# Row-sum reciprocals of two 16-head attentions: four iterative reciprocals, or a guess by exponential and two corrections

## The chip, the cores and the metric

The kernel runs on 1 core of a Trainium2 chip. The metric is the device time of one execution in microseconds. TensorE is called PE in the views, VectorE DVE, ScalarE ACT, GpSimd POOL and SyncE SP.

## What is computed

Four layers in sequence on `x` of 4 sequences x 1024 tokens x 128 features. Each ends with `x = layernorm(x + layer(x))`. Layer 0 is a causal attention of 16 heads of 64, layer 1 an attention of 8 heads whose weights are gated (top 3 of 5 experts), layer 2 an attention of 16 heads with a bias by relative position, layer 3 a mixture of 16 experts. The change is in layers 0 and 2 alone, and there in the denominators of the softmax:

```python
def _L0_attn_ref(x, W_Q, W_K, W_V, W_O):
    ...
    masked = jnp.where(causal, scores, jnp.float32(-MASK_VAL))
    attn = jax.nn.softmax(masked / np.float32(np.sqrt(D_HEAD)), axis=-1)
    z = jnp.einsum('bacC,baCh->bach', attn, v)
    out = jnp.einsum('aeh,bach->bce', W_O, z)
    return out
def _L1_attn_ref(hidden_states, Wq, Wk, Wv, Wo, rel_bias):
    ...
    scores = jnp.einsum('bqhd,bkhd->bhqk', q, k) * SM_SCALE + bias
    attn = jax.nn.softmax(scores, axis=-1)
    out = jnp.einsum('bhqk,bkhd->bqhd', attn, v).reshape(b, s, H * DK)
    return out @ Wo
```

All arithmetic is in fp32. Products that need its precision are made of two halves (`ah` and `al`, `bh` and `bl`) in fp32r.

## The kernel before, in words

`pair_stage` runs layers 0 and 2, called s0 (causal) and s2 (biased) here; `gated_stage`, s1, runs between them, and the experts come last. A stage treats 32 pairs of heads: 4 sequences x 8 pairs. A pair has units `(c, j)`: query half `c` of 512 columns, key block `j` of 128. There are 16 units a pair in s2 and 12 in s0 (blocks over the diagonal are left out, and later ones are narrower). All units of one `c` are a pass, so each stage has 64 passes, numbered `s = 2g + c`.

Each engine runs its part of the same list of units in order, and semaphores tie them together. In a unit

- TensorE makes the scores of two heads in PSUM (`sT`, two buffers, L359 and L364), one or two blocks of products for the row maxima of the next pair (`mx`, one buffer, L340), and the product of the probabilities of two units before with the values (`pv`, L384). Jobs that share the single bank `misc` lie between: projections of the next pairs ("item", "v"), the column sums ("rs"), transposes and the output projection ("y"). A job waits until the last one's `misc` has been read (`misc_free`);
- VectorE reads the maxima (`maxima`: L548 and L551 in s0; L561 and L567 in s2), subtracts halves (L527) and, in s2, adds the near biases in PSUM before the exponential (`near_biases`, L610, units 0 to 4 and 11 to 15). Next come, where a pair's maxima are complete, their rows (L577 to L595);
- ScalarE takes the exponential of the scores (`exponentials`, L476) into one of four buffers `prob`, and copies PSUM to SBUF (`copy`, L426);
- POOL adds up the exponentials of a pass elementwise (L729), SBUF to SBUF, and in s0 masks the diagonal block (L714).

The denominator of a pass: when POOL has added the last unit, TensorE multiplies `psum_p` with ones into `misc` ("rs", L286), so that each of 128 partitions holds the sums of its head; ScalarE copies them into `recip` (L426); VectorE takes the reciprocal in four pieces of 128 columns, one a unit, at the start of the unit (`reciprocals`, L615), and later multiplies the copied `pv` in `z` with it (`normalize`, L621). `Pairs.jobs` writes the order: for the second pass of the pair before, "rs" is in unit 2, the reciprocals in units 3 to 6 and the product in unit 7; for a pair's own first pass they are in units `at1+2`, `at1+3` to `at1+6` and the next or last unit, where `at1` is 4 in s0 and 8 in s2 (so 10, 11 to 14 and 15 in s2). `y`, the output projection, waits for `z_done` once a sequence.

The order of the work is in these lists alone; nothing is planned at run time.

## Time and profile before

| | |
|---|---|
| runs | 4654.91, 4660.39 (median), 4664.32 us |
| profiled execution, its own time | 4659.69 us |
| its span in the profile | 4658.0 us |
| mean granted clock of TensorE | 0.946 |
| TensorE busy | 4061.7 us (87%) |
| VectorE busy | 3451.8 us (74%) |
| POOL busy | 2799.3 us (60%) |
| ScalarE busy | 1968.4 us (42%) |

By the exponentials at L476, s0's units run from 94 to 1281 us and s2's from 2807 to 4477 us. "Pair 12" below is the thirteenth of its stage; its first unit starts at 3436.7 us in s2.

How to read the views: the stretches give the time in which an engine had an instruction running. The view of the waits tells whose result ended an engine's idle time. The groups sum all instructions of one line, operation and tile: busy time, mean length of one, and idle time just before them. The view in time merges neighbours of one engine that are alike (x2, x3). What is recorded as the start of a VectorE or POOL instruction can lie before it moves data, so an instruction that waits for memory reads as a long one.

### The profile page before, as it was taken

The page shows a single profiled execution, that of the slowest core. Times are in us where ns is not written, and L with a number is a line of the kernel's source. Part 1 is how long each engine was busy: PE and PEld are TensorE (multiplying, and loading weights), DVE is VectorE, ACT ScalarE, POOL GpSimd, SP SyncE. Part 2 cuts the span into 40 slices and gives each one's busy share as a digit, 9 for nine tenths or more (in the row PEclk, how much of TensorE's full clock was granted, in tenths as well). Part 3 has the DMA queues.
Part 4 walks back from the last instruction along what each step waited for, and adds up shares of the span by engine and source line. Part 5 has one row for each costly group of instructions (what it writes and reads, how often), then busy time and mean ns, then how long its engine had stood idle before and what let it go on. Part 6 is the DMA issues. An engine that isn't in the chain of part 4 may idle for free. (4 is left out here: it accounts for less than half of the span.)

```text
span 4658.0 us, 63371 instructions
## 1 busy us (share of the span) xinstructions
PE 4061.7 (87%) x22554; PEld 2155.1 (46%) x22554; DVE 3451.8 (74%) x5816; ACT 1968.4 (42%) x3446; POOL 2799.3 (60%) x2036
## 2 busy tenths in 40 slices
PE   5999999999968889989899748999999999999964
PEld 3554544444444555555555324444444444444423
DVE  3777887868757777777877537887888788878836
ACT  2443443434434555455454313443444344434422
POOL 0655655646624777777887905665666566656640
PEclk6999999999978999999999959999999999999987
DMA  3000000000010000000000021211122121212111
GB/s 51 14 14 14 23 14 23 14 9 6 1 63 26 26 26 26 27 26 26 31 26 9 5 59 27 39 28 28 37 35 34 28 37 28 34 23 44 18 46 37
DMA packets 98041, 125.90 MB, mean 27 GB/s; under 512 B 28896, under 2 KB 76448, under 8 KB 97728
## 3 DMA queue, kind: packets, MB, share of 16 engines
q1 hardware_dynamic: 97728, 121.86, 12.2%
q8 instruction: 180, 2.95, 0.3%
q14 instruction: 133, 1.09, 0.1%
HBM read 103.69 MB, written 18.12 MB: 26 GB/s over the span
## 5 line engine op out<-in xcount | busy, mean ns | idle before, releaser
L729 POOL TENSOR_TENSOR s_psum_p<-s_psum_p,s_prob 128x1024 f32<-128x1024 f32 (+3 forms) x640 | 1350.0, 2109 | 418.9 <-ACT s_prob L476 379.9
L476 ACT ACTIVATE s_prob<-s_sT 128x1024 f32<-128x1024 f32 (+2 forms) x896 | 835.9, 933 | 969.5 <-DVE s_sT L610 477.3
L384 PE MATMUL s_pv<-s_prob,s_vp 128*64 128x512 f32 (+3 forms) x3584 | 890.4, 575 | 3.9 <-POOL s_prob L714 2.9
L729 POOL TENSOR_TENSOR s_psum_p<-s_prob 128x1024 f32<-128x1024 f32 (+1 forms) x128 | 286.9, 2241 | 574.7 <-ACT s_prob L476 572.1
L615 DVE RECIPROCAL s_recip<-s_recip 128x128 f32<-128x128 f32 x512 | 481.3, 942 | 100.3 <-ACT s_recip L426 100.3
L340 PE MATMUL s_mx<-s_bh,s_ah 64*128 64x512 f32 (+3 forms) x1792 | 390.1, 431 | 184.1 <-DVE s_bm L551 85.3
L1613 POOL TENSOR_TENSOR s_psum_p<-s_psum_p,s_prob 128x1024 f32<-128x1024 f32 x192 | 461.5, 2403 | 107.5 <-ACT s_prob L1336 105.5
L561 DVE CUSTOM_DVE_ANT_0 s_mx<-s_mx,s_strip 128x512 f32<-128x512 f32 x640 | 429.4, 712 | 111.8 <-PE s_mx L340 110.7
L1336 ACT ACTIVATE s_prob<-s_sT 128x1024 f32<-128x1024 f32 x256 | 262.4, 1025 | 583.8 <-PE s_sT L1200 583.7
L359 PE MATMUL s_sT<-s_ah,s_bh 64*128 64x512 f32 (+3 forms) x1792 | 414.5, 459 | 19.1 <-ACT s_prob L476 18.8
L551 DVE TENSOR_REDUCE s_bm<-s_mx 128x8 f32<-128x1024 f32 (+3 forms) x384 | 362.5, 944 | 50.5 <-PE s_mx L340 41.7
L1449 DVE SCALAR_TENSOR_TENSOR s_part<-s_sT,s_gate,s_part 128x128 f32<-128x128 f32 x945 | 287.6, 322 | 131.0 <-ACT s_part L1328 81.2
L340 PEld LDWEIGHTS s_mx<-s_bh,s_ah 64*128 64x128 f32 x1792 | 172.9, 189 | 415.3 <-DVE s_bm L551 165.6
L1493 DVE TENSOR_REDUCE s_bm<-s_mx 128x2 f32<-128x1024 f32 x214 | 261.5, 1222 | 136.6 <-PE s_mx L1165 135.7
L359 PEld LDWEIGHTS s_sT<-s_ah,s_bh 64*128 64x128 f32 x1792 | 168.8, 185 | 398.0 <-issue 217.2
L359 PE MATMUL s_sT<-s_al,s_bh 64*128 64x512 f32 (+3 forms) x1792 | 339.5, 374 | 0.0
L359 PE MATMUL s_sT<-s_ah,s_bl 64*128 64x512 f32 (+3 forms) x1792 | 339.0, 374 | 0.0
L364 PE MATMUL s_sT<-s_mr,s_rowsel 64*128 64x512 f32 (+3 forms) x1792 | 338.8, 373 | 0.0
L567 DVE TENSOR_REDUCE s_bm<-s_mx 128x2 f32<-128x1024 f32 x192 | 232.7, 1212 | 102.3 <-PE s_mx L340 101.9
L384 PEld LDWEIGHTS s_pv<-s_prob,s_vp 128*64 128x64 f32 x3584 | 178.1, 135 | 254.7 <-issue 223.9
L610 DVE TENSOR_TENSOR s_sT<-s_sT,s_near 128x512 f32<-128x512 f32 (+2 forms) x320 | 236.5, 739 | 65.0 <-PE s_sT L364 64.7
L1212 PE MATMUL s_pv<-s_prob,s_qkv 128*64 128x512 f32 x1024 | 280.8, 628 | 2.6 <-ACT s_z L1257 2.6
(251 smaller groups left out, 7535.9 us busy)
## 6 DMA issues: line engine op xcount, KB each, us to landing
s_strip<-bias_rows SPq DMA_DIRECT2D x256, 144.0 KB, 5.8
s_wr<-gated_weights SPq DMA_DIRECT2D x32, 960.0 KB, 4.8
s_near<-bias_rows SPq DMA_DIRECT2D x256, 48.0 KB, 2.0
x<-s_x SPq DMA_DIRECT2D x12, 512.0 KB, 3.2
s_x<-x SPq DMA_DIRECT2D x8, 512.0 KB, 4.8
gated_weights<-s_side_hi SPq DMA_DIRECT2D x8, 480.0 KB, 2.5
gated_weights<-s_side_lo SPq DMA_DIRECT2D x8, 480.0 KB, 2.9
s_x<-in_L_attn_x_dram SPq DMA_DIRECT2D x4, 512.0 KB, 4.6
```

The costliest lines, as they stand in the source:

```text
L340: last = mm(mx[:, hd, 0:hi], ah[heads(hd), g % 3, i * P:(i + 1) * P], bh[heads(hd), g % 3, c * CH:c * CH + hi], start=True, stop=True)
L359: mm(sT[:, k % 2, hd, lo:CH], key[heads(hd), r, keys], query[heads(hd), r, cols], start=n == 0, stop=False)
L364: last = mm(sT[:, k % 2, hd, lo:CH], rowsel[heads(hd), j if st.biased else 0, :], mr[heads(hd), g % 2, cols], start=False, stop=True)
L384: last = mm(pv[heads(hd), lo:CH], vp[:, g % 2, j, heads(hd)], prob[:, k % PR, hd, lo:CH], start=j == 0, stop=end)
L476: nc.scalar.activation(prob[:, k % PR, :, lo:CH], sT[:, k % 2, :, lo:CH], ACT.Exp, scale=st.scale).then_inc(exp_done, 1)
L551: nc.vector.tensor_reduce(bm[:, g % 2, :, i, 4 * c:4 * c + nblk], mx[:, :, 0:nblk * P].rearrange("p a (j n) -> p a j n", n=P), X, ALU.max)\
L561: last = nc.vector.tensor_tensor_reduce(out=mx[:, hd, :], in0=mx[:, hd, :], in1=strip[:, g % 2, hd, first:first + CH], scale=1.0, scalar=N ...
L615: nc.vector.reciprocal(cols, cols).then_inc(recip_done, 1)
L729: nc.gpsimd.tensor_tensor(out[:, :, lo:CH], src, p[:, :, lo:CH], ALU.add)\
L1212: last = mm(pv[heads(hd), :], qkv[:, g % 3, j, 2, heads(hd)], prob[:, k % PR, hd, :], start=j == 0, stop=j == NB - 1)
L1449: nc.vector.scalar_tensor_tensor(o, src, scale(s, e), o if e else more[:, to], ALU.mult, ALU.add).then_inc(p_dve, 1)
L1613: nc.gpsimd.tensor_tensor(out, src, p, ALU.add).then_inc(sum_done, 1)
```

## The change

`recip` still gets the sums by a copy. Right behind it ScalarE takes a guess of their reciprocals from the same bank: it reads the bits of the fp32 sums as an integer and takes `exp(127 ln 2 - 0.03 - ln 2 · bits / 2^23)`, which is 2 to the negative of a piecewise linear logarithm. With `t` the sum and `r` the guess, VectorE makes `t·r` (n0), ScalarE `(t·r - 1.5)²` (`squares`), VectorE `r·(square + 0.75)` (n1), `-t·r` (n2), `z·r` (n3) and `z·(2 - t·r)` (n4). All are whole passes of 128x512. `guess` and `square` have one buffer each. The bank `misc` is free for TensorE's next job after the guess (`guess_done`) and no more after the copy (`rs_read`). In the unit VectorE's reciprocal work now comes behind the near biases, the maxima and their rows. n0 is in the unit of the first reciprocal before, the square in the unit behind it, n1 and n2 in the second unit behind, n3 and n4 in the third. Two memsets set the bias columns `shifts`.

```diff
--- before.py
+++ after.py
@@ jobs
         for s, u in ((2 * g - 1, 3), (2 * g, rs1 + 1)):
             if s >= 0:
-                for n in range(4):
-                    out[u + n].append(("recip", s, n))
-                out[u + 4 if u + 4 < self.U else u + 3].append(("norm", s))
+                for n, later in enumerate((0, 2, 2, 3, 3)):
+                    out[u + later].append(("recip", s, n))
+                out[u + 1].append(("sq", s))
@@ tensor, misc_free
                 elif kind == "rs":
-                    pe.wait_ge(rs_read, of + 1)
+                    pe.wait_ge(guess_done, of + 1)
@@ scalar, misc_job
                     copy(recip[:, s % 2, :], misc[:, :]).then_inc(rs_read, 1)
+                    if s == 0:
+                        act.wait_ge(shift_set, 2)
+                    else:
+                        act.wait_ge(recip_done, 3 * s)
+                    nc.scalar.activation(guess[:, :], misc[:, :].bitcast(I32), ACT.Exp,
+                                         scale=-math.log(2.0) / 2 ** 23, bias=shifts[:, 0:1])\
+                        .then_inc(guess_done, 1)
@@ scalar
+            def squares(s):
+                act.wait_ge(near_one, s + 1)
+                nc.scalar.activation(square[:, :], square[:, :], ACT.Square, bias=shifts[:, 1:2])\
+                    .then_inc(sq_done, 1)
+
@@ scalar, units
                     if t[0] in MISC:
                         misc_job(t)
+                    elif t[0] == "sq":
+                        squares(t[1])
@@ vector
             def reciprocals(s, n):
-                dve.wait_ge(rs_read, s + 1)
-                cols = recip[:, s % 2, n * P:(n + 1) * P]
-                nc.vector.reciprocal(cols, cols).then_inc(recip_done, 1)
-
-            def normalize(s):
-                dve.wait_ge(recip_done, 4 * (s + 1))
-                dve.wait_ge(pv_read, s + 1)
-                out = z[:, (s // 2) % NZ, half(s % 2)]
-                tt(out, out, recip[:, s % 2, :], ALU.mult).then_inc(z_done, 1)
+
+                total, r, out = recip[:, s % 2, :], guess[:, :], z[:, (s // 2) % NZ, half(s % 2)]
+                fused = nc.vector.scalar_tensor_tensor
+                if n == 0:
+                    dve.wait_ge(rs_read, s + 1)
+                    dve.wait_ge(guess_done, s + 1)
+                    tt(square[:, :], total, r, ALU.mult).then_inc(near_one, 1)
+                elif n == 1:
+                    dve.wait_ge(sq_done, s + 1)
+                    fused(r, square[:, :], 0.75, r, ALU.add, ALU.mult).then_inc(recip_done, 1)
+                elif n == 2:
+                    dve.wait_ge(recip_done, 3 * s + 1)
+                    fused(total, total, -1.0, r, ALU.mult, ALU.mult).then_inc(recip_done, 1)
+                elif n == 3:
+                    dve.wait_ge(pv_read, s + 1)
+                    tt(out, out, r, ALU.mult).then_inc(recip_done, 1)
+                else:
+                    dve.wait_ge(recip_done, 3 * s + 3)
+                    fused(out, total, 2.0, out, ALU.add, ALU.mult).then_inc(z_done, 1)
@@ vector, units
             for g, u, k, c, j, todo in units():
-                for t in todo:
-                    if t[0] == "recip":
-                        reciprocals(t[1], t[2])
                 if st.near(c, j):
                     near_biases(k)
                 for t in late:
                     misc_job(t)
@@
-                    elif t[0] == "norm":
-                        normalize(t[1])
+                    elif t[0] == "recip":
+                        reciprocals(t[1], t[2])
```

At the end of a stage the last pass runs the same steps with nothing between them.

How the order of VectorE moves, at two places of a pair of s2. Names are the program's tiles; the ISA rows are reads of `mx`. First from the end of unit 4's read of `mx` to the first of unit 6's, before:

```order
L561 ISA s_bm 128x1
L615 RECIPROCAL s_recip<-s_recip 128x128
L567 TENSOR_REDUCE s_bm<-s_mx 128x2
L615 RECIPROCAL s_recip<-s_recip 128x128
L527 TENSOR_TENSOR s_bl<-s_misc,s_bh 128x512
L561 ISA s_mx,s_bm<-s_mx,s_strip 128x512
```

And now, where L583 and L589 read the maxima, L549 subtracts, and L641, L644, L647 are n0, n1, n2:

```order
L583 ISA s_bm 128x1
L589 TENSOR_REDUCE s_bm<-s_mx 128x2
L644 SCALAR_TENSOR_TENSOR s_guess<-s_square,s_guess 128x512
L647 SCALAR_TENSOR_TENSOR s_recip<-s_recip,s_guess 128x512
L549 TENSOR_TENSOR s_bl<-s_misc,s_bh 128x512
L583 ISA s_mx,s_bm<-s_mx,s_strip 128x512
```

The two reciprocals of units 5 and 6 are gone, and n1 and n2 stand together behind unit 5's read, ahead of unit 6's subtraction. Second the end of unit 12 to unit 15, before:

```order
L577 COPY s_m<-dcol 128x2x16
L581 TENSOR_TENSOR s_bm<-s_bm,delta 128x2x3
L586 TENSOR_REDUCE s_m<-s_bm 128x2x8
L615 RECIPROCAL s_recip<-s_recip 128x128
L610 TENSOR_TENSOR s_sT<-s_sT,s_near 128x2x384
L615 RECIPROCAL s_recip<-s_recip 128x128
L610 TENSOR_TENSOR s_sT<-s_sT,s_near 128x2x384
L595 TENSOR_TENSOR s_mr<-s_mx,constants 128x512 x2
L610 TENSOR_TENSOR s_sT<-s_sT,s_near 128x2x256
L621 TENSOR_TENSOR s_z<-s_z,s_recip 128x512
L610 TENSOR_TENSOR s_sT<-s_sT,s_near 128x2x256
```

And now, with the near biases at L632, the rows of maxima at L617 and n3, n4 at L650, L653:

```order
L599 COPY s_m<-dcol 128x2x16
L603 TENSOR_TENSOR s_bm<-s_bm,delta 128x2x3
L608 TENSOR_REDUCE s_m<-s_bm 128x2x8
L632 TENSOR_TENSOR s_sT<-s_sT,s_near 128x2x384
L644 SCALAR_TENSOR_TENSOR s_guess<-s_square,s_guess 128x512
L647 SCALAR_TENSOR_TENSOR s_recip<-s_recip,s_guess 128x512
L632 TENSOR_TENSOR s_sT<-s_sT,s_near 128x2x384
L617 TENSOR_TENSOR s_mr<-s_mx,constants 128x512 x2
L650 TENSOR_TENSOR s_z<-s_z,s_guess 128x512
L653 SCALAR_TENSOR_TENSOR s_z<-s_recip,s_z 128x512
L632 TENSOR_TENSOR s_sT<-s_sT,s_near 128x2x256 x2
```

The near biases of units 13 and 14 no more stand behind a reciprocal; n1 and n2 stand between those two, and n3 and n4 between the rows of maxima and unit 15's near bias, where the product stood behind that one.

## Rows read from the trace of the kernel before

**Rows 1.** Stretches s0 and s2: busy us of each engine, clock, DMA share, GB/s.
```profile
94.00:1282.00 1188.00, 1092.18 (x6865) 582.48 (x6864) 914.59 (x1189) 505.53 (x712) 700.11 (x607) 0.98 0.04 13
2807.00:4477.00 1670.00, 1564.65 (x8655) 731.17 (x8655) 1353.55 (x2368) 710.99 (x832) 1078.86 (x450) 1.00 0.19 30
```

**Rows 2.** TensorE in s0, s2: waiter <- releaser, us in all, times, longest.
```profile
PE s_mx L340 <- DVE s_bm L551: 75.8, 102, 1.4
...
PE s_mx L340 <- DVE s_bm L561: 54.2, 96, 1.0
PE s_mx L340 <- DVE s_bm L567: 22.5, 52, 1.6
PE s_sT L359 <- ACT s_prob L476: 18.8, 31, 1.6
```

**Rows 3.** Groups of VectorE, first s0, then s2 (busy us, mean ns | idle before).
```profile
L621 DVE TENSOR_TENSOR s_z<-s_z,s_recip 128x512 f32<-128x512 f32 x63 | 93.7, 1487 | 0.0
...
L615 DVE RECIPROCAL s_recip<-s_recip 128x128 f32<-128x128 f32 x252 | 237.9, 944 | 38.6 <-ACT s_recip L426 38.6
...
L621 DVE TENSOR_TENSOR s_z<-s_z,s_recip 128x512 f32<-128x512 f32 x63 | 85.3, 1354 | 0.0
```

**Rows 4.** Line 621 in s2: durations of one in ns, least, median, greatest.
```profile
L621 DVE TENSOR_TENSOR s_z<-s_z,s_recip x63: 680/1679/2590, 2855.2 to 4475.6; 128x512 f32<-128x512 f32 x63
```

**Rows 5.** In time, s2 pair 12, units 5 to 7: VectorE, then POOL (start, us).
```profile
3452.57 1.16 DVE L567 TENSOR_REDUCE s_bm<-s_mx 128x2 f32<-128x1024 f32 x1
...
3455.70 0.70 DVE L561 CUSTOM_DVE_ANT_0 s_mx<-s_mx,s_strip 128x512 f32<-128x512 f32 x1
...
3460.32 0.73 DVE L561 CUSTOM_DVE_ANT_0 s_mx<-s_mx,s_strip 128x512 f32<-128x512 f32 x1
...
3460.97 1.69 DVE L621 TENSOR_TENSOR s_z<-s_z,s_recip 128x512 f32<-128x512 f32 x1
...
3451.08 4.90 POOL L729 TENSOR_TENSOR s_psum_p<-s_psum_p,s_prob 128x1024 f32<-128x1024 f32 x2 [0.27 <-ACT s_prob L476]
3456.57 2.37 POOL L729 TENSOR_TENSOR s_psum_p<-s_psum_p,s_prob 128x1024 f32<-128x1024 f32 x1 [0.60 <-ACT s_prob L476]
3459.74 2.37 POOL L729 TENSOR_TENSOR s_psum_p<-s_psum_p,s_prob 128x1024 f32<-128x1024 f32 x1 [0.79 <-ACT s_prob L476]
```

**Rows 6.** Groups of VectorE in s1: scalar-tensor-tensor of 128 and 64 columns.
```profile
L1449 DVE SCALAR_TENSOR_TENSOR s_part<-s_sT,s_gate,s_part 128x128 f32<-128x128 f32 x567 | 198.5, 350 | 124.3 <-ACT s_part L1328 81.2 <-PE s_sT L1135 28.3 <-POOL s_qkv L1626 1.3
...
L1449 DVE SCALAR_TENSOR_TENSOR s_part<-s_sT,s_gate,s_part 128x64 f32<-128x64 f32 x378 | 105.7, 280 | 6.7
```

**Rows 7.** In time, s1: three operations on VectorE, then two on POOL.
```profile
1504.66 0.55 DVE L1468 TENSOR_TENSOR s_beats<-s_gate 128x384 f32<-128x384 f32 x1
...
1749.02 2.75 DVE L1468 TENSOR_TENSOR s_beats<-s_gate 128x384 f32<-128x384 f32 x1
1751.80 1.12 DVE L1470 TENSOR_TENSOR s_keep<-s_keep,s_beats 128x384 f32<-128x384 f32 x1
...
1748.37 2.97 POOL L1613 TENSOR_TENSOR s_psum_p<-s_psum_p,s_prob 128x1024 f32<-128x1024 f32 x1
1751.30 1.21 POOL L1639 TENSOR_TENSOR s_gsum<-s_gsum,s_prod 128x320 f32<-128x320 f32 x1
```

**Rows 8.** Waits of POOL in s2.
```profile
POOL s_psum_p L729 <- ACT s_prob L476: 663.9, 317, 98.3
```

**Rows 9.** In time, pair 12 of s2, units 14 and 15, VectorE, then POOL.
```profile
3484.70 1.27 DVE L595 TENSOR_TENSOR s_mr<-s_mx,constants 128x512 fp32r<-128x512 f32 x2
3485.90 0.69 DVE L610 TENSOR_TENSOR s_sT<-s_sT,s_near 128x512 f32<-128x512 f32 x1
...
3484.22 5.19 POOL L729 TENSOR_TENSOR s_psum_p<-s_psum_p,s_prob 128x1024 f32<-128x1024 f32 x2 [3.18 <-ACT s_prob L476]
```

**Rows 10.** Groups of ScalarE in the whole span.
```profile
L426 ACT ACTIVATE s_recip<-s_misc 128x512 f32<-128x512 f32 x128 | 76.5, 598 | 159.5 <-PE s_misc L286 159.5
...
L1336 ACT ACT_TABLE_LOAD x7 | 9.0, 1283 | 0.1
```

More of the change, by code:

```diff
@@ L13 @@
+import math
 from contextlib import ExitStack
@@ L21 @@
 U32 = mybir.dt.uint32
+I32 = mybir.dt.int32
 ALU = mybir.AluOpType
@@ L183, in pair_stage @@
         recip = sb("recip", [P, 2, CH])
+        guess = sb("guess", [P, CH])
+        square = sb("square", [P, CH])
+        shifts = sb("shifts", [P, 2])
         x2 = sb("x2", [P, 2, NB, D])
@@ L211, in pair_stage @@
         recip_done, z_done = sem("recip_done"), sem("z_done")
+        guess_done, near_one, sq_done, shift_set = (sem(n) for n in ("guess_done", "near_one", "sq_done",
+                                                                     "shift_set"))
         y_full, yT_done, t_full, res_done = sem("y_full"), sem("yT_done"), sem("t_full"), sem("res_done")
@@ L507, in _ @@
             misc_job(("rs", 2 * GP - 1))
+            squares(2 * GP - 1)
             for c in range(2):
@@ L656, in _ @@
             nc.vector.memset(m8[:, :, :, :], 0.0).then_inc(set_up, 1)
+            nc.vector.memset(shifts[:, 0:1], 127.0 * math.log(2.0) - 0.03).then_inc(shift_set, 1)
+            nc.vector.memset(shifts[:, 1:2], -1.5).then_inc(shift_set, 1)
             for c in range(2):
@@ L691, in _ @@
                 late = [t for t in todo if t[0] in MISC]
-            s = 2 * GP - 1
-            for n in range(4):
-                reciprocals(s, n)
-            normalize(s)
+            for n in range(5):
+                reciprocals(2 * GP - 1, n)
             for c in range(2):
```

## The prediction

> **What bounds the kernel now.** I read the stretches first, because the change touches only the two 16-head stages, s0 (causal) and s2 (biased). [rows 1] give TensorE 1092 of 1188 us busy in s0 and 1565 of 1670 in s2: 92 and 94%, at a granted clock of 0.98 and 1.00, so 2.4 GHz. VectorE is the second engine, 915 and 1354 us, which leaves it 273 and 316 us idle, 589 in all; ScalarE is busy 43% in both. So the most that anything can win here is TensorE's idle time, 96 + 105 = 201 us.
>
> Next the waits of TensorE [rows 2]. It waits for VectorE's read of the maxima tile `mx` for 75.8 us in s0 and 54.2 + 22.5 us in s2: `mx` has one buffer, so TensorE's next maxima stand behind VectorE's read of the last. It waits 18.8 us for exponentials in s2. That is 171 of the 201 us. VectorE isn't full, but in places TensorE already runs at its pace, and lateness there is paid at once.
>
> Then the operations that the change replaces [rows 3]. A pass (half a pair; 64 per stage) has four reciprocals of 0.944 us, 3.78 us, and one product `z`·`recip` of 1.487 us in s0 and 1.354 us in s2, mean 1.42. Its extremes [rows 4] are the row that decides this case: the same 128x512 product takes 0.680 us at best, 1.679 in the median and 2.590 at worst. Whatever stretches it is shown by the pieces in time: in [rows 5] POOL's add begins at 3459.74 and takes 2.37 us; the product that VectorE begins at 3460.97 takes 1.69 us and ends at 3462.66, 0.55 us behind the add. The reads at L561, which have one operand in SBUF and one in PSUM, keep their 0.70 to 0.73 us during the same add. So a VectorE operation with both operands in SBUF stands still while POOL works on SBUF. (The Trainium skill, "SBUF — State Buffer", section "Who interferes with whom", has this as a rule: a VectorE instruction with two SBUF inputs contends with a GpSimd one that reads SBUF, and whoever starts first keeps the port to its end. The trace agrees, with the 0.680 and 2.590 us above.)
>
> **The change, part by part.** Each pass loses four reciprocals, which read one operand and never wait, and gets five operations of 128x512 in place of the single product, all with two operands in SBUF: n0 (total·guess), n1 (correction), n2 (total·r negated), n3 (z·r), n4 (second correction).
>
> Bare price on VectorE: two tensor-tensor at 0.68. Three scalar-tensor-tensor are not in the trace at this width; [rows 6] give 0.350 us for 128 columns and 0.280 for 64, 1.09 ns a column, so 0.77 us at 512 (lower bound 0.68, as the product). Together 1.36 + 2.31 = 3.67 us, against 3.78 + 1.42 = 5.20. Without waits the change saves 1.5 us a pass, 3.0 a pair.
>
> Waits. The product's mean wait is 1.42 - 0.68 = 0.74 us; I give that to n0, n1 and n3. n2 and n4 stand directly behind n1 and n3. What happens to such a row of dependent two-SBUF operations is shown in s1 [rows 7]: L1468 begins at 1749.02 behind POOL's L1613 (to 1751.34) and takes 2.75 us, where 0.55 is its bare time (at 1504.66); POOL's next, L1639, is recorded from 1751.30 and takes 1.21; VectorE's next, L1470, of the same width, takes 1.12. The engines alternate: between two VectorE operations POOL gets its turn, if it has one ready. POOL's adds in s0 and s2 are 2.4 us each, and in s2 317 of 448 (14 a pair) waited for their exponential [rows 8], so three in ten were ready at once. I take n2 and n4 to meet one half of the time, 1.2 us each (bounds: never, 0, and always, 2.4). A pass is then 3.67 + 3·0.74 + 2·1.2 = 8.3 us, 3.1 more than before. 126 of the passes lie beside other work: +390 us of VectorE time, of the 589 that it has idle. Bounds: -190 us (no wait at all) and, all five meeting a whole add, 3.67 + 5·2.4 = 15.7 us a pass, more than there is room for.
>
> How much reaches TensorE. Two places of one pair of s2, by its own times. Units 5 and 6 [rows 5]: the read at L567 begins at 3452.57 and ends at 3453.73. n1 comes next, and POOL's second add holds to 3455.98; n1 ends near 3456.7; the add that followed at 3456.57 is ready, and n2 ends near 3459.7. The subtraction and the read of `mx` that began at 3455.70 come behind it, some 4 us late (the reciprocals that go save nothing of that, since the read at L567 waits for TensorE), and TensorE waits for that read. Units 14 and 15 [rows 9]: the rows of maxima (L595) end at 3485.97. n3 meets an add that ends near 3486.6 and ends at 3487.3; the second add was ready (the row has both in 5.19 us, without a gap) and holds to 3489.7; n4 ends near 3490.4. Only then comes the near bias that began at 3485.90. It is 4.5 us late, less the 1.9 us of two reciprocals that stood ahead of it: 2.6. Together 6 to 7 us a pair if nothing is made good, 200 us over s2's 32 pairs. In s0 the places are alike but several of POOL's pieces are shorter, so I take half to two thirds, 100 to 130 us. Since a late exponential makes POOL idle and takes the next conflict away, and VectorE has slack in the units with long projections, I let 0.6 of the 390 us reach the end: **+234 us**.
>
> What it gives back: near biases come first in units 3 to 6 and 11 to 14, up to 0.94 us earlier. That bears on the 18.8 us of waits for exponentials; I take half, -10 us. New on ScalarE: the guess and the square of 128x512. The copy of that shape takes 0.598 us [rows 10]; for the bias by column and the source in SBUF I put 0.1 on top (bounds 0 and 0.2). That is 1.4 us x 128 = 179 us on an engine idle for 57% of both stages. The guess stands behind the copy of the same sums and ahead of the next exponential; in s2 the latter then waits for its near bias anyway. The square stands a unit after n0, so n0 is over when its turn comes; behind it wait at most a copy and the next exponential, for two units ahead. `misc` is held 0.7 us longer, but the next job there is a unit away, 3.3 us in the mean of s2 (1670 us over 512 units). I cost these three at nothing; were every guess exposed, it would be 128·0.7 = 90 us. At each stage's end nothing hides the chain: now 3.8 us of reciprocals and 0.68; then guess 0.7, n0 0.68, square 0.7 and n1 to n4, 3.0: 5.1 us. +0.6 us a stage; with the new hand-overs between the two engines I say +2 for both. The two memsets: nothing.
>
> Sum: 4659.7 (the profiled execution's own time, 0.7 us under the median of 4660.4) + 234 - 10 + 2 = 4886; I say **4885 us**.
>
> **The rivals.**
> *Faster: VectorE finds POOL idle.* The five begin as POOL's add is released, or earlier by 0.1 us, and nearly always win. Price: 3.0 us a pair less on VectorE, at the very places where TensorE waits 152 us for it. If a third of that and half of the exponentials' 18.8 goes, the time is 4600 us. For it: products that met no add and took 0.680, and POOL idle 35 to 41% of both stages (700 and 1079 us busy [rows 1]). Against: a median of 1.679. It decides if the mean of the five is under 1.04 us (5.20/5). 17%, of which the part from 4635 to 4650 is one in four.
> *VectorE's idle time swallows most.* 200 us would remain to it even after +390. Then only 20 to 130 us show: 4670 to 4790. For it: 19 to 23% idle now. Against: the waits lie where it has none. 14%. Between the two lies the case without difference (within 0.2%, about what a measurement of this kernel can tell), 5%.
> *Worse: nearly every n2 and n4 pays a whole add and nothing is made good:* 400 us or more, over 5060. 6%.
> *Another ACT table for the square.* (The Trainium skill, "ScalarE: Activation LUTs", section "Table sets: the hidden batching unit", says that every switch between sets of functions costs a load of a set.) A load takes 1.283 us in s1 [rows 10]; two a pass would be 128·2·1.283 = 328 us, 4990. The order of the changed kernel has no load more than before, so this gets no more than 1%, in the forecast's range.
>
> **How the numbers follow.** Forecast with its own range 4790 to 5060: 58%, the table case in it. Swallowed: 14%. Same: 5%. Worse than 5060: 6%. Faster: 17%. The range 4635 to 5060 leaves out 13 + 6%. Faster by over 0.2% 0.17, within 0.05, slower 0.78.
>
> **What would show it.** The five groups on VectorE with means over 1.2 us and maxima near 3.1, n2 and n4 above n1 and n3; POOL's add longer than its 2.4 us in the mean; TensorE's waits for `mx` well over 152 us; ScalarE up by 179 us; VectorE's busy time up, not down. Wrong I am if n1 to n4 come out near 0.7 to 0.9 us, or if TensorE's idle time in s0 and s2 stays at 201 us while VectorE's grows.

## The result, and the profile after

The changed kernel takes 4980.31 us (median of 4 runs, 4975.27 to 4983.44) against 4660.68 us for the one before in the same comparison: 1.0682 times as long, 95% interval 1.0668 to 1.0697, or 320 us more. Forecast was 4885 us in a range of 4635 to 5060, with 0.78 for slower. The side and the range held; the size was too small by 95 us.

First the stretches of the two stages, s0 and s2, whose columns are those of [rows 1]:

```profile
94.00:1416.00 1322.00, 1151.94 (x6863) 606.18 (x6861) 1039.05 (x1186) 575.23 (x838) 725.62 (x606) 0.93 0.04 11
2944.00:4801.00 1857.00, 1628.72 (x8655) 755.43 (x8657) 1485.23 (x2369) 778.08 (x958) 1120.49 (x451) 0.96 0.16 27
```

Both stages are longer, by 134 and 187 us, together 321: everything lies here. VectorE is busy 125 and 132 us more than in [rows 1]. TensorE's part splits in two. Its idle time (length less busy time) rises from 96 to 170 us and from 105 to 228, +197 in all. And it is *busy* 60 and 64 us more with the same matmuls, +124, because the granted clock is lower: 0.93 and 0.96 in place of 0.98 and 1.00. (1092 x 0.98/0.93 is 1151 and 1565 x 1.00/0.96 is 1630, against 1152 and 1629 measured.)

Next the waits of TensorE in s0 and then in s2, as in [rows 2]: waiter, releaser, us in all, times, longest.

```profile
PE s_mx L347 <- DVE s_bm L573: 124.0, 96, 3.7
...
PE s_mx L347 <- DVE s_bm L583: 93.9, 79, 3.6
PE s_sT L366 <- ACT s_prob L490: 84.4, 59, 3.1
PE s_mx L347 <- DVE s_bm L589: 22.9, 54, 1.6
```

The waits for the maxima tile `mx` grow from 75.8 to 124.0 us in s0 and from 54.2 to 93.9 in s2. They are no more frequent than in [rows 2] (96 against 102 times, 79 against 96), but the longest is 3.6 or 3.7 us in place of 1.4 and 1.0. The wait for exponentials goes from 18.8 to 84.4 us: they come late because VectorE adds the near biases late. One case, at units 14 and 15 of pair 12 of s2, as the view in time has it: n4 (L653) holds back the near biases (L632), ScalarE's exponential waits for these, and TensorE for the exponential.

```profile
3692.61 2.75 DVE L653 SCALAR_TENSOR_TENSOR s_z<-s_recip,s_z 128x512 f32<-128x512 f32 x1
...
3695.28 1.28 DVE L632 TENSOR_TENSOR s_sT<-s_sT,s_near 128x512 f32<-128x512 f32 x2
...
3696.00 1.94 ACT L490 ACTIVATE s_prob<-s_sT 128x1024 f32<-128x1024 f32 x2 [4.29 <-DVE s_sT L632]
...
3697.08 0.50 PE L366 MATMUL s_sT<-s_ah,s_bh 64*128 64x512 f32 x2 [1.97 <-ACT s_prob L490]
```

The five new operations, n0 (L641) to n4 (L653), first in s0, then in s2 (busy us, mean ns of one | idle before):

```profile
L644 DVE SCALAR_TENSOR_TENSOR s_guess<-s_square,s_guess 128x512 f32<-128x512 f32 x63 | 128.0, 2032 | 2.6 <-ACT s_square L495 2.6
L641 DVE TENSOR_TENSOR s_square<-s_recip,s_guess 128x512 f32<-128x512 f32 x63 | 102.3, 1624 | 5.2 <-ACT s_guess L447 5.2
L647 DVE SCALAR_TENSOR_TENSOR s_recip<-s_recip,s_guess 128x512 f32<-128x512 f32 x62 | 101.9, 1644 | 2.1
L653 DVE SCALAR_TENSOR_TENSOR s_z<-s_recip,s_z 128x512 f32<-128x512 f32 x62 | 53.6, 865 | 2.1
L650 DVE TENSOR_TENSOR s_z<-s_z,s_guess 128x512 f32<-128x512 f32 x62 | 52.4, 845 | 0.0
...
L647 DVE SCALAR_TENSOR_TENSOR s_recip<-s_recip,s_guess 128x512 f32<-128x512 f32 x63 | 109.8, 1743 | 2.2
L641 DVE TENSOR_TENSOR s_square<-s_recip,s_guess 128x512 f32<-128x512 f32 x63 | 107.2, 1701 | 0.0
L653 DVE SCALAR_TENSOR_TENSOR s_z<-s_recip,s_z 128x512 f32<-128x512 f32 x63 | 105.2, 1670 | 2.2
L650 DVE TENSOR_TENSOR s_z<-s_z,s_guess 128x512 f32<-128x512 f32 x63 | 55.9, 888 | 0.0
L644 DVE SCALAR_TENSOR_TENSOR s_guess<-s_square,s_guess 128x512 f32<-128x512 f32 x63 | 50.0, 793 | 1.8 <-ACT s_square L495 1.7
```

The five means add up to 7.01 us a pass in s0 and 6.80 in s2, against the 5.20 of [rows 3]. A mean hides that in s2 there are mostly two kinds. The lengths of n0 and n2 in s2, least, median and greatest in ns:

```profile
L641 DVE TENSOR_TENSOR s_square<-s_recip,s_guess x63: 679/2630/2901, 2981.0 to 4785.0; 128x512 f32<-128x512 f32 x63
...
L647 DVE SCALAR_TENSOR_TENSOR s_recip<-s_recip,s_guess x63: 691/2720/2839, 2989.6 to 4790.8; 128x512 f32<-128x512 f32 x63
```

An operation there is bare (nothing holds it up, 0.68 to 0.69 us), or stands about 2 us behind one of POOL's adds. And the place decides which. Taken apart by the two passes of a pair, n0 in s2 has a mean of 2.67 us in the one and 0.70 in the other, n2 0.96 and 2.55, n4 2.55 and 0.76. So three long stalls come in nearly every pair of s2, at the same places. In s0, where some of POOL's pieces are shorter, four places are long: n0 (2.52 us) and n1 (1.87) in the one pass, n1 (2.20) and n2 (2.47) in the other.

Pair 12 of s2 in time: VectorE in units 5 and 6 with what waits for it, then POOL over the same stretch.

```profile
3654.86 1.23 DVE L589 TENSOR_REDUCE s_bm<-s_mx 128x2 f32<-128x1024 f32 x1 [0.59 <-PE s_mx L347]
...
3656.00 0.68 DVE L644 SCALAR_TENSOR_TENSOR s_guess<-s_square,s_guess 128x512 f32<-128x512 f32 x1
...
3656.72 2.75 DVE L647 SCALAR_TENSOR_TENSOR s_recip<-s_recip,s_guess 128x512 f32<-128x512 f32 x1
...
3659.39 0.68 DVE L549 TENSOR_TENSOR s_bl<-s_misc,s_bh 128x512 fp32r<-128x512 f32 x1
3659.99 0.68 DVE L583 CUSTOM_DVE_ANT_0 s_mx<-s_mx,s_strip 128x512 f32<-128x512 f32 x1
...
3661.44 0.79 PE L347 MATMUL s_mx<-s_bh,s_ah 64*128 64x512 f32 x2 [2.35 <-DVE s_bm L583]
...
3656.01 5.66 POOL L758 TENSOR_TENSOR s_psum_p<-s_psum_p,s_prob 128x1024 f32<-128x1024 f32 x2
```

Here is the stall of [rows 5] made long. n1 and POOL's add start together at 3656.00 and n1 is bare; n2, directly behind it, takes 2.75 us. The adds pay too: two take 5.66 us, where one alone in [rows 5] takes 2.37, and two together 4.90. The subtraction and the read of `mx` stand behind n2, and TensorE stands still for 2.35 us. The prediction walked these very units and had n2 long there, but n1 held up as well.

What the clock does after that, in stretches of 4 us (columns as above):

```profile
3656.00:3660.00 4.00, 3.09 (x17) 1.29 (x16) 3.96 (x5) 1.62 (x2) 3.84 (x2) 1.00 0.00 0
3660.00:3664.00 4.00, 2.56 (x12) 1.75 (x12) 3.11 (x10) 0.02 (x1) 1.68 (x1) 0.66 0.00 0
3664.00:3668.00 4.00, 4.00 (x21) 1.83 (x23) 2.98 (x8) 1.90 (x3) 2.39 (x1) 0.91 0.01 2
3668.00:3672.00 4.00, 3.76 (x26) 2.31 (x24) 2.48 (x5) 1.53 (x3) 0.00 (x0) 1.00 0.01 2
```

The granted clock is 1.00 (2.4 GHz) while TensorE idles for these 2.35 us, then 0.66 in the mean of 4 us, a part of them at the lower level of 1.2 GHz, and 1.00 again at 3668. Meanwhile one 64x512 score matmul takes 0.63 us instead of 0.40. In the same pair of the kernel before, no stretch of 4 us in units 0 to 15 falls below 1.00.

Last, ScalarE's two new groups and its loads of tables:

```profile
L495 ACT ACTIVATE s_square<-s_square,s_shifts 128x512 f32<-128x512 f32 x128 | 91.7, 716 | 3.6 <-DVE s_square L641 3.6
L447 ACT ACTIVATE s_guess<-s_misc,s_shifts 128x512 f32<-128x512 int32 x128 | 87.5, 684 | 94.9 <-DVE s_z L650 94.9
...
L1365 ACT ACT_TABLE_LOAD x7 | 9.0, 1283 | 0.1
```

Together 179.2 us, as costed; no table load more (7 on this line, as in [rows 10]). The guess waits 94.9 us for n3 of the pass before, which releases its one buffer: all of it in s0.

### The profile page after: what moved, and what is told of

It is laid out like the page before. It is cut to its first block and busy times, and to the rows that moved or that the text cites. A ratio compares the mean times of both kernels' runs of the same rounds, so it can differ in the third digit from the quotient of the medians.

```text
span 4981.7 us, 63639 instructions
## 1 busy us (share of the span) xinstructions
PE 4187.6 (84%) x22554; PEld 2204.6 (44%) x22554; DVE 3710.2 (74%) x5820; ACT 2109.0 (42%) x3702; POOL 2867.6 (58%) x2036
## 5 line engine op out<-in xcount | busy, mean ns | idle before, releaser
L758 POOL TENSOR_TENSOR s_psum_p<-s_psum_p,s_prob 128x1024 f32<-128x1024 f32 (+3 forms) x640 | 1403.6, 2193 | 623.5 <-ACT s_prob L490 587.0
L391 PE MATMUL s_pv<-s_prob,s_vp 128*64 128x512 f32 (+3 forms) x3584 | 940.9, 605 | 10.3 <-ACT s_prob L490 5.4
L347 PE MATMUL s_mx<-s_bh,s_ah 64*128 64x512 f32 (+3 forms) x1792 | 409.7, 453 | 283.5 <-DVE s_bm L573 133.5
L366 PE MATMUL s_sT<-s_ah,s_bh 64*128 64x512 f32 (+3 forms) x1792 | 427.3, 473 | 84.4 <-ACT s_prob L490 84.4
L583 DVE CUSTOM_DVE_ANT_0 s_mx<-s_mx,s_strip 128x512 f32<-128x512 f32 x640 | 428.8, 711 | 87.9 <-PE s_mx L347 86.8
L371 PE MATMUL s_sT<-s_mr,s_rowsel 64*128 64x512 f32 (+3 forms) x1792 | 352.2, 388 | 8.4 <-DVE s_mr L617 8.4
L366 PE MATMUL s_sT<-s_ah,s_bl 64*128 64x512 f32 (+3 forms) x1792 | 350.9, 387 | 0.0
L366 PE MATMUL s_sT<-s_al,s_bh 64*128 64x512 f32 (+3 forms) x1792 | 350.3, 387 | 0.0
L589 DVE TENSOR_REDUCE s_bm<-s_mx 128x2 f32<-128x1024 f32 x192 | 234.7, 1222 | 136.3 <-PE s_mx L347 136.0
L632 DVE TENSOR_TENSOR s_sT<-s_sT,s_near 128x512 f32<-128x512 f32 (+2 forms) x320 | 236.8, 748 | 115.2 <-PE s_sT L371 115.2
L743 POOL TENSOR_SCALAR_AFFINE_SELECT s_prob<-s_prob 128x256 f32<-128x256 f32 x256 | 131.6, 514 | 293.0 <-ACT s_prob L490 292.4
```

The costliest lines, as they stand in the source:

```text
L347: last = mm(mx[:, hd, 0:hi], ah[heads(hd), g % 3, i * P:(i + 1) * P], bh[heads(hd), g % 3, c * CH:c * CH + hi], start=True, stop=True)
L366: mm(sT[:, k % 2, hd, lo:CH], key[heads(hd), r, keys], query[heads(hd), r, cols], start=n == 0, stop=False)
L371: last = mm(sT[:, k % 2, hd, lo:CH], rowsel[heads(hd), j if st.biased else 0, :], mr[heads(hd), g % 2, cols], start=False, stop=True)
L391: last = mm(pv[heads(hd), lo:CH], vp[:, g % 2, j, heads(hd)], prob[:, k % PR, hd, lo:CH], start=j == 0, stop=end)
L583: last = nc.vector.tensor_tensor_reduce(out=mx[:, hd, :], in0=mx[:, hd, :], in1=strip[:, g % 2, hd, first:first + CH], scale=1.0, scalar=N ...
L758: nc.gpsimd.tensor_tensor(out[:, :, lo:CH], src, p[:, :, lo:CH], ALU.add)\
```

## The experiments

What is open: whether the loss is VectorE's time, ScalarE's part, the new order, the single guess buffer, POOL's lengthened adds, or a few long stalls; and what the forecast's "0.6 reaches the end" should have been. Differences below are read from the ratios to the kernel before (x 4660). Where the text says so, a kernel leaves work out. Gains and losses under 0.2% are not told from none.

**e1, one operand each.** Each of the five becomes a reciprocal of 92 columns, which reads one operand and takes about as long as a bare operation. The division by the row sums is left out.

```diff
-                    tt(square[:, :], total, r, ALU.mult).then_inc(near_one, 1)
+                    nc.vector.reciprocal(square[:, 0:92], total[:, 0:92]).then_inc(near_one, 1)
...
```

> The changed kernel, in which each of the five VectorE operations of a pass is a reciprocal of 92 columns: the same place, semaphores and about the same bare length (0.69 us), but one operand in SBUF. It leaves out the normalisation. Theory C (operations with two SBUF operands stand still while POOL works): the five take 0.68 to 0.72 us each with no spread, TensorE's waits for the maxima fall back to 150 us or less, its clock recovers, and the time is 4600 to 4660 us. Theory O (the new order and the chain over ScalarE are at fault, whatever the operands): it stays over 4900 us.

Measured: 4640.05 us, ratio 0.9950 (0.9934 to 0.9967). The five take 0.71 to 0.73 us each, 3.6 a pass; TensorE idles 80 us in s0 and 97 in s2. Its waits for `mx`, s0 and then s2:

```profile
PE s_mx L347 <- DVE s_bm L573: 61.6, 73, 1.4
...
PE s_mx L347 <- DVE s_bm L583: 53.9, 92, 1.4
PE s_mx L347 <- DVE s_bm L589: 23.2, 55, 1.5
```

So without the stalls the loss is gone whole, ScalarE's work and all hand-overs included. But 1.6 us less a pass than before, 200 us of VectorE time, gain 23 us only, and all of it in s0: 1172 us for 1188, while s2 has 1671 for 1670. Of the 152 us of waits for `mx` 139 remain. Whether they are the same waits isn't shown, since e1 has the new order too.

**e2, the order alone.** The kernel before, with its reciprocals behind the unit's near biases and maxima.

```diff
-                for t in todo:
-                    if t[0] == "recip":
-                        reciprocals(t[1], t[2])
...
+                    elif t[0] == "recip":
+                        reciprocals(t[1], t[2])
```

> The kernel before, with its four reciprocals behind the near biases and the maxima of their unit in place of ahead of them. C: no two-SBUF operation is added, so 4630 to 4670 us, a gain of 10 us or so by earlier exponentials. O: if the place behind the maxima is at fault, 4800 us or more.

Measured: 4693.31 us, ratio 1.0060 (1.0043 to 1.0077), 28 us more. The wait for exponentials doesn't fall (16 us against 18.8), and the product meets POOL more often; in s2 its least, median and greatest are now

```profile
L621 DVE TENSOR_TENSOR s_z<-s_z,s_recip x62: 1580/1742/2630, 2863.1 to 4485.5; 128x512 f32<-128x512 f32 x62
```

where [rows 4] have 680, 1679 and 2590. The loss is mostly in s2, 1695 us for 1670 (s0: 1195 for 1188), where TensorE's waits for `mx` rise from 76.7 to 92.3 us. The product there now takes 1.91 us in the mean, for 1.35. So the new place of the reciprocals is a loss; how much of it comes by way of the longer product is not separated.

**e3, ScalarE alone.** The kernel before, with the guess and the square added on ScalarE, and `misc` released by the guess. Nothing uses their results.

```diff
-                    pe.wait_ge(rs_read, of + 1)
+                    pe.wait_ge(guess_done, of + 1)
...
+                    nc.scalar.activation(guess[:, :], misc[:, :].bitcast(I32), ACT.Exp,
...
+                nc.scalar.activation(guess[:, :], guess[:, :], ACT.Square, bias=shifts[:, 1:2])\
```

> The kernel before plus ScalarE's part of the change alone: the guess (nobody reads it) behind the copy of the sums, the square a unit behind the first reciprocal, misc released by the guess. C: 4655 to 4690 us; ScalarE's 179 us lie in its idle time. Theory S (ScalarE's additions and the longer hold of misc cost): 4750 us or more.

Measured: 4654.48 us, ratio 0.9989 (0.9979 to 0.9998). ScalarE's part and the longer hold of `misc` cost nothing. (The square doesn't wait for VectorE here; that hand-over is in e1.)

**e4, two guesses.** The changed kernel with two guess buffers in s0, so that the guess no longer waits for n3 of the pass before.

```diff
-        guess = sb("guess", [P, CH])
+        NG = 2 if st.causal else 1
+        guess = sb("guess", [P, NG, CH])
```

> The changed kernel with two buffers of the guess in s0. The trace of the changed kernel shows the guess of s0's first pass 4 us late, since it waits for the pass before to finish with the one buffer. Theory G (that wait holds up exponentials and sums): 4920 to 4950 us. If it lies in TensorE's wait for VectorE anyway: 4970 to 4985 us.

Measured: 5006.31 us, ratio 1.0734 (1.0716 to 1.0752): 24 us *slower* than the changed kernel, and all of that in s0 (1346 us). The groups of n0 and n3 in s0:

```profile
L651 DVE TENSOR_TENSOR s_z<-s_z,s_guess 128x512 f32<-128x512 f32 x62 | 74.0, 1194 | 0.0
L642 DVE TENSOR_TENSOR s_square<-s_recip,s_guess 128x512 f32<-128x512 f32 x63 | 55.3, 877 | 5.1 <-ACT s_guess L448 5.1
```

n0 falls from 1.62 to 0.88 us, n3 rises from 0.85 to 1.19, and the stage gets longer though the five together get shorter (6.6 us a pass, from 7.0). The single buffer is not the cause. In the odd passes n3 now takes 1.55 us for 0.86, TensorE's waits for `mx` in s0 rise from 124.0 to 139.3 us and the granted clock falls from 0.93 to 0.91. Why a stall there weighs more than one at n0 isn't settled.

**e5, apart.** As e4, with n2, n3 and n4 each one unit later, so that no operation stands directly behind another except n3 and n4.

```diff
-                for n, later in enumerate((0, 2, 2, 3, 3)):
+                for n, later in enumerate((0, 2, 3, 4, 4)):
```

> The changed kernel with two guesses in s0 (5006 us), and n2 a unit after n1, n3 and n4 another unit later. Theory A (engines alternate: n2 pays a whole add because it stands directly behind n1): n2 of the second passes falls from 2.5 to under 1.5 us and the time by 30 to 80 us. Rival P (what an operation pays is set by where in the unit it stands, next to the end of the exponential that releases an add, not by what is ahead of it): single operations pay as well, the sum of the five stays about 7 us, and the time stays within 30 us of 5006.

Measured: 4997.13 us, ratio 1.0716 (1.0692 to 1.0741), which overlaps with e4. In s2 the stalls move: in a pair's first pass n2, n3 and n4 now take 1.36, 2.26 and 2.73 us in the mean (0.96, 1.02 and 2.55 in the changed kernel), and in the other pass n2 falls from 2.55 to 0.80. The five add up to 7.3 us a pass in s2, for 6.8, and the stage takes 1869 us for 1857; s0 takes 1322, 24 less than in e4 and the same as in the changed kernel. Taking the pairs apart buys nothing as a whole. It also moves the waits in s2: those for exponentials fall from 84.4 to 29.3 us, now that n4 stands behind unit 15's near biases, and those for `mx` rise from 116.8 to 167.4.

**e6, short adds.** The changed kernel, with POOL's adds from the third unit of a pass on made 8 columns wide. It leaves out most of the adding up of exponentials, and nothing on VectorE.

```diff
                     pool.wait_ge(sum_done, st.summed(k) - 1)
+                    lo = CH - 8
                     src = out[:, :, lo:CH]
```

> The changed kernel, VectorE's five operations with two SBUF operands left as they are, but all of POOL's adds from the third unit of a pass on are 8 columns a head wide in place of 512: the sums leave most of the probabilities out. Theory C (the wait is for POOL): the five operations fall to 0.7 us in nearly all places and the time to 4620 to 4680 us. If two SBUF operands were slow for another reason, they keep 1.4 us in the mean and the time stays over 4900.

Measured: 4641.59 us, ratio 0.9953 (0.9934 to 0.9971). The stretches of s0 and s2, then POOL's adds and VectorE's five in s2:

```profile
94.00:1291.00 1197.00, 1097.31 (x6865) 586.52 (x6867) 865.58 (x1189) 573.37 (x838) 351.95 (x609) 0.97 0.04 13
2815.00:4460.00 1645.00, 1561.58 (x8654) 729.86 (x8655) 1221.16 (x2368) 782.56 (x958) 272.94 (x451) 1.00 0.19 31
...
L759 POOL TENSOR_TENSOR s_psum_p<-s_psum_p,s_prob 128x16 f32<-128x16 f32 x384 | 115.9, 302 | 980.6 <-ACT s_prob L490 976.4
...
L647 DVE SCALAR_TENSOR_TENSOR s_recip<-s_recip,s_guess 128x512 f32<-128x512 f32 x63 | 43.6, 692 | 2.2
L653 DVE SCALAR_TENSOR_TENSOR s_z<-s_recip,s_z 128x512 f32<-128x512 f32 x63 | 43.6, 691 | 2.2
L641 DVE TENSOR_TENSOR s_square<-s_recip,s_guess 128x512 f32<-128x512 f32 x63 | 43.2, 685 | 0.0
L650 DVE TENSOR_TENSOR s_z<-s_z,s_guess 128x512 f32<-128x512 f32 x63 | 43.1, 684 | 0.0
L644 DVE SCALAR_TENSOR_TENSOR s_guess<-s_square,s_guess 128x512 f32<-128x512 f32 x63 | 43.0, 682 | 1.7 <-ACT s_square L495 1.7
```

All five are unchanged instructions with two operands in SBUF, and all are bare once POOL's adds are short. e1 took the stalls away on VectorE's side and e6 on POOL's, and either way the loss is gone. That both end at 4640 us is chance: e6 has 9 us more in s0 than the kernel before, where n1 of the odd passes still takes 2.20 us (the first two adds of a pass are whole there), and 25 us less in s2, where TensorE's waits for exponentials are gone too and POOL has 806 us less to do than before; e1 has its gain in s0. (The Trainium skill, "SBUF — State Buffer", section "Who interferes with whom", has the rule that a VectorE instruction with two SBUF inputs contends with a GpSimd one that reads SBUF. With e6 it is shown here by an intervention: n0 takes 1701 ns beside whole adds and 685 beside short ones.)

**e7, same lengths, and e8, even lengths.** One-operand reciprocals in the place of the five again, so that nothing waits for POOL, but long ones. In e7 each place of each pass gets a length of its own, meant to be that of the changed kernel; they came out 7 to 10% short, 6.4 us a pass. In e8 the same sum is spread evenly, 1.28 us each. Both leave out the division.

```diff
+                w = (((357, 87, 118, 129, 340), (90, 119, 340, 98, 98)) if st.biased else ((336, 246, 105, 107, 126), (89, 293, 329, 112, 98)))[s % 2][n]
...
-                    tt(square[:, :], total, r, ALU.mult).then_inc(near_one, 1)
+                    nc.vector.reciprocal(square[:, 0:w], total[:, 0:w]).then_inc(near_one, 1)
```

e8 has `w = 178 if st.biased else 184`.

> As the one-operand kernel of 4640 us, but each reciprocal has as many columns as make it as long as the operation in its place was in the mean in the changed kernel (0.7 to 2.7 us, by stage and by first or second pass). It leaves out the normalisation. If the loss is all lateness of VectorE, it comes back: 4930 to 4990 us, with the clock down to 0.92. If POOL's own delay, or what else the shared memory access does, has a part, it stays under 4900.

> As before, with the same sum of VectorE time, but all five equally long (1.36 us). Theory B (few long stalls at the wrong places do it: three a pair of 2.2 to 2.7 us): well under the kernel with the lengths as measured, 4700 to 4850 us. If the sum alone counts: within 30 us of it.

Measured: e7 4899.53 us, ratio 1.0520 (1.0486 to 1.0554); e8 4866.94 us, ratio 1.0443 (1.0421 to 1.0465). With no stall behind POOL at all, VectorE time alone brings 205 to 240 us. That the time comes in few long pieces adds some 35 us, by the stretches all of it in s2 (1815 us for 1786; s0 has 1268 for 1272); most of it is the sum.

**e10, true lengths.** e7 with the numbers of columns corrected (381 for 336, 404 for 357, and so on). It leaves out the division.

> The changed kernel, with each of the five operations made a one-operand reciprocal whose number of columns gives it the mean length that the operation of that pass and place has in the changed kernel (7.0 us a pass in s0, 6.8 in s2); e7 had meant the same, but its lengths came out 7 to 10% short. This leaves out the division by the row sums. If the whole loss lies in VectorE being held for so long at these places, and the operations' second operand does nothing else: 4950 to 4985 us, as the changed kernel's 4980, and TensorE idle about 165 us in s0 and 225 in s2. If a part of the loss comes by another way (POOL's adds, which the changed kernel makes 0.09 us longer in s2, or exponentials behind them), the time stays at 4900 to 4940 us.

Measured: 4959.48 us, ratio 1.0629 (1.0613 to 1.0646). Stretches of s0 and s2:

```profile
94.00:1399.00 1305.00, 1148.02 (x6865) 606.19 (x6864) 1028.33 (x1189) 574.28 (x838) 682.65 (x607) 0.93 0.04 12
2933.00:4788.00 1855.00, 1627.18 (x8653) 753.75 (x8651) 1479.90 (x2368) 778.93 (x958) 1068.31 (x450) 0.96 0.17 27
```

In s2 this is the changed kernel again, 1855 against 1857 us with the same idle time and clock, though POOL is busy 1068 us in place of 1120. In s0, 17 us are missing (1305 against 1322), with POOL at 683 instead of 726 us. This execution took 4974.87 us, 15 over e10's median, so the rest of 25 us can't be laid to one stage by it. I put the rest down to POOL's adds being stretched, by argument only. The bulk of the loss is time on VectorE at these places.

**e11, the sum of before.** As e8 with `w = 143`: 1.04 us each, 5.2 us a pass, what the four reciprocals and the product cost before. It leaves out the division.

> The changed kernel's order, with each of the five operations a one-operand reciprocal of 143 columns, 1.04 us, so that a pass costs VectorE 5.2 us, as the four reciprocals and the product do in the kernel before. It leaves out the division by the row sums. Known so far: 3.6 us a pass gives 4640 us, 6.4 us a pass 4867. If the loss grows in proportion to the sum: a straight line through these two gives 4770 us at 5.2 us a pass. If there is a knee where VectorE begins to hold TensorE, and the kernel before stands just under it: 4660 to 4710 us, with what the new places cost (e2 had +31 for the order alone) in it.

Measured: 4742.13 us, ratio 1.0158 (1.0141 to 1.0175). Stretches of s0 and s2:

```profile
94.00:1315.00 1221.00, 1110.77 (x6865) 594.22 (x6863) 928.62 (x1188) 574.32 (x838) 683.14 (x607) 0.96 0.04 12
2842.00:4560.00 1718.00, 1579.82 (x8652) 734.35 (x8651) 1382.73 (x2368) 779.43 (x958) 1068.31 (x450) 0.99 0.18 30
```

That is between the straight line (4770) and the knee (4660 to 4710), and decides for neither. The new places cost more than the 28 us of e2: with the same 5.2 us a pass the kernel before takes 74 us less.

**e9 and e12, the product one unit later.** The kernel before, with `z`·`recip` of a pair's odd passes in unit 8 in place of 7; e9 in s2 alone, e12 in both stages. Nothing is left out.

```diff
-                out[u + 4 if u + 4 < self.U else u + 3].append(("norm", s))
+                later = 5 if u == 3 and not after else 4
+                out[u + later if u + later < self.U else u + 3].append(("norm", s))
```

e9 has `self.biased and` ahead of `u == 3`.

> The kernel before, with one thing moved: in s2 the product z times recip of a pair's odd passes comes one unit later, with unit 8 in place of 7. It leaves nothing out. If the long product (1.68 us in the mean there) holds up the subtraction and the read of the maxima behind it in unit 7, where TensorE waits some 0.5 us a pair, and unit 8 has room: 4640 to 4655 us. If the place only changes which unit pays: 4655 to 4665 us. If it meets a fresh add of POOL there in most pairs: 4670 to 4700 us.

> As e9, in s0 too, where the odd product takes 2.15 us in the mean. It leaves nothing out. If the late unit has more room in both stages: 4625 to 4650 us. If only the place changes: 4655 to 4665 us. If it meets a fresh add there: 4670 us and more, and the mean of the odd products in s0 rises to 2.4 us or over.

Measured: e9 4662.46 us, ratio 1.0000 (0.9989 to 1.0011); e12 4653.33 us, ratio 0.9973 (0.9959 to 0.9987). The product in s2 in e9 and in s0 in e12:

```profile
L622 DVE TENSOR_TENSOR s_z<-s_z,s_recip x62: 676/682/2590, 2866.0 to 4463.5; 128x512 f32<-128x512 f32 x62
```

```profile
L622 DVE TENSOR_TENSOR s_z<-s_z,s_recip x63: 675/774/2345, 126.5 to 1263.4; 128x512 f32<-128x512 f32 x63
```

The stall is gone, in s2 a median of 682 for 1679 ns, and the time in s2 doesn't move (1671 us for 1670): that stall cost nothing. In s0 the odd product falls from 2.15 to 0.92 us in the mean and the stage from 1188 to 1174 us, but TensorE's waits for `mx` there stay at 75.0 us for 75.8, and in e9, with s0 untouched, the same stage took 1192 us. How e12 gains is not shown. It is the only complete kernel of this study that is faster than the one before by more than 0.2%: 0.27%.

## Why the prediction was right about the side and short in the size

The 320 us (318 by the ratio), taken apart by a ladder of runs; its first step still changes several things at once:

| step | what differs | us |
|---|---|---|
| before to e11 | new order and places, ScalarE's part; 5.2 us a pass in both | +74 |
| e11 to e10 | 5.2 to 6.9 us a pass, in the long pieces that the stalls make | +220 |
| e10 to the change | second operands, and with them POOL's longer adds | +25 |

- **The bare price** was 0.69, not 0.77 us for a scalar-tensor-tensor of 512 columns: the lower bound was right, the slope of [rows 6] too steep. Five bare operations cost 3.4 us a pass, not 3.67.
- **The waits.** The mechanism held: two operands in SBUF, POOL first, VectorE still, and n2 long in units 5 and 6 and n4 (2.75 us) in 14 and 15, as walked. The price did not: a chance for each place was the wrong model. n1 in s2 (0.79) and n3 in both stages (0.85, 0.89) were nearly bare, n0 (1.62, 1.70) was not, and in s0 n4 was (0.87). The sum is 6.9 us a pass, not 8.3: by the lengths of the records, as the forecast counted, 212 us more than before in all, not 390. (VectorE's busy time grew by 256, since neighbouring records overlapped more before.)
- **The share that reaches the end** is the step that failed. The text took 0.6. Measured, TensorE's idle time alone grew by 197 us, 0.93 of the 212, and the whole loss is 1.5 of them. In the order of the changed kernel, from e11 to e10, 215 us more of VectorE brought 220. The stalls sit where `mx` or a near bias is wanted next, and slack elsewhere made little good. The walk through single units came closer than the share that replaced it: it gave 200 us in s2 and 100 to 130 in s0, measured 187 and 134. That is luck in part, for the walk had only idle time in it, and of the 187 us 64 are slower matmuls.
- **The clock** had no term at all. The +124 us of TensorE busy time in the same matmuls is more than the 95 us that the forecast was short by. Before, TensorE was idle for 8 and 6% of the two stages at a clock of 0.98 and 1.00; after, for 13 and 12% at 0.93 and 0.96.
- **The near biases first**, forecast at -10 us, went the other way: e2, the order alone, is at +28 with its longer products in it, and the wait for exponentials became 84 us, since n4 now stands ahead of the *next* near bias. The walk through units 14 and 15 had said so without drawing the sum, and e5, with n4 behind that bias, has 29 us of this wait.
- **ScalarE, `misc`, tables**: 179 us as costed, on the path nothing (e3), no load more. The end of the stage was right: in s2 from the end of the copy of the sums at 4805.69 to n4's end at 4810.59 is 4.9 us, forecast 5.1.
- **The signs** named beforehand came out in the main: in s2 POOL's add grew to 2.51 us in the mean, and the waits for `mx` to 241 us. But the greatest lengths were 2.9 us, not 3.1, in each stage three of the five means lay over 1.2 us and not all, and n2 above n1 and n4 well above n3 hold in s2 alone.
- **The faster rival** was priced wrong even on its own condition. e1 gives it everything it asks, five operations of 0.71 to 0.73 us (and e6 in s2, with 0.68 to 0.69), and the time is 4640, not 4600: of the 152 us of waits for `mx` a third was to go, and 9% went (e1, in the new order; of the 18.8 us of waits for exponentials 8.0 are left there). "Swallowed by idle time" fell: with VectorE idle for 20% of both stages, nothing of the step from e11 to e10 was sheltered.

So the closeness of 4885 to 4980 is luck in part: too much VectorE time (390 for 212) and too little of it counted at the end (0.6 for 1.5) cancelled in the main.

The share is no constant either. Within the order of the changed kernel, with one-operand operations of even length:

| us a pass | time (ratio x 4660) | slope, share of 126 passes |
|---|---|---|
| 3.6 (e1) | 4637 | |
| 5.2 (e11) | 4734 | 61 us per us a pass: 0.5 |
| 6.4 (e8) | 4866 | 110: 0.9 |

Of the time up to 5.2 us a pass half is hidden, of what comes above it little.

Open: why two guess buffers make s0 longer (e4); how the +74 of the first step divides beyond the 28 of the order; and how much of the clock's fall comes from each stall. The sum of TensorE's idle time doesn't tell it: in e1 it is less than before (80 and 97 us for 96 and 105), and the granted clock is lower all the same (0.96 and 0.99 for 0.98 and 1.00).

## What to carry to other kernels

Before one-operand work is traded for two-operand work on VectorE, look at what POOL does beside it: here five bare 0.69 us operations became 6.9 us a pass, and shortening POOL's adds or taking the second operand away removed the whole loss. A stall belongs to a place in the order: find the place, and who is queued behind it. The product's stall of about 1 us in s2 cost nothing (e9); the stalls ahead of `mx` and of the near biases cost about their whole length (220 us for 215, e11 to e10). And where a change adds to TensorE's idle time, read the granted clock as well: here its fall was 124 of 320 us.

## What was not expected of the hardware

- Stalls are not spread at random: in s2 n0 takes 2.67 us in one pass of each pair and 0.70 in the other, through 32 pairs.
- The conflict lengthens both sides: POOL's two adds beside n1 and n2 take 5.66 us together, 2.83 each, where one alone takes 2.37.
- Not every pause of TensorE lowers its clock. After the 2.35 us ahead of 3661.44 the granted clock was 0.66 over 4 us; after the 1.97 us ahead of 3697.08, it stayed at 1.00:

```profile
3692.00:3696.00 4.00, 3.10 (x17) 1.31 (x15) 3.97 (x4) 0.00 (x0) 2.66 (x2) 1.00 0.00 0
3696.00:3700.00 4.00, 2.92 (x18) 1.56 (x20) 3.55 (x8) 3.11 (x4) 2.40 (x1) 1.00 0.35 85
```

- A reciprocal's length goes by its columns: 0.72 us for 92 columns and 2.67 for 404, which is 6.25 ns a column; a scalar-tensor-tensor of 512 columns takes 0.69.
